# Adaptive-norm double layer: statistics closed ahead of the two joints, last tile gated by VectorE, and a drain with TensorE transposes and split tiles

## The reference

```python
h = layernorm(x) * (1 + ca) + sa;  x = x + ga * attn0(h)   # 32 heads of 16, softmax over the heads of one token
h = layernorm(x) * (1 + cb) + sb;  x = x + gb * ffn0(h)    # base + top-2 of 16 LoRA experts
h = layernorm(x) * (1 + ca1) + sa1; x = x + ga1 * attn1(h) # latent attention: 32 heads, 2 batches
h = layernorm(x) * (1 + cb1) + sb1; x = x + gb1 * ffn1(h)
# ffn1: eff_W = W + lora_B @ lora_A
#       y = h @ eff_W.T / sqrt(sum(eff_W**2, axis=1)) * magnitude
# layernorm: (x - mean) / sqrt(var + 1e-5); ga.., gb.. are pushed to at least 0.25 in magnitude
```

## Time and profile before

| what | value |
|---|---|
| time, median of 3 runs | 903.19 us (901.45 to 907.17) |
| the profiled execution | 899.29 us, span 897.1 us |
| TensorE busy | 816.5 us, 91% |
| VectorE busy | 681.6 us, 76% |
| ScalarE busy | 535.0 us, 60% |
| GpSimd busy | 538.9 us, 60% |
| block 0 ends, block 1 starts | 155.6 / 155.9 us |
| block 1 ends, block 2 starts | 283.8 / 284.1 us |
| last scores (step 255) | 838.9 us |
| mean granted TensorE clock | 0.967 of 2.4 GHz |

### The profile page before, as it was taken

One profiled execution on the slowest core, in us unless ns is written; L12 is line 12 of the kernel. 1 busy time (PEld: TensorE's weight loads), 2 busy tenths in 40 slices (PEclk: granted clock), 3 DMA queues, 4 the chain that ended last, 5 costly groups with the idle time before them and its releaser, 6 DMA issues.

```text
span 897.1 us, 15066 instructions
## 1 busy us (share of the span) xinstructions
PE 816.5 (91%) x4560; PEld 537.7 (60%) x4560; DVE 681.6 (76%) x1322; ACT 535.0 (60%) x1158; POOL 538.9 (60%) x481
## 2 busy tenths in 40 slices
PE   3899994899995997899999999999999999999997
PEld 1588873667774874565656565655656556565543
DVE  4768896835443477989989898889998889898652
ACT  5668874733323775666666666665666666665522
POOL 3333432021222237998989888887888888897213
PEclk8899997899997998999999999999999999999999
DMA  8630000494424442666666666665566766565511
GB/s 330 216 122 2 1 2 3 133 245 152 128 68 152 124 130 50 162 159 155 155 150 156 152 155 152 157 155 139 141 155 183 187 150 156 145 159 138 133 33 70
DMA packets 91459, 120.07 MB, mean 134 GB/s; under 512 B 30386, under 2 KB 41650, under 8 KB 91380
## 3 DMA queue, kind: packets, MB, share of 16 engines
q1 hardware_dynamic: 66804, 85.54, 34.5%
q10 hardware_dynamic: 24576, 33.59, 15.2%
HBM read 41.45 MB, written 2.10 MB: 49 GB/s over the span
## 4 chain that ended last, share of the span: by engine, by line
PE 42%; DVE 9%; issue 6%; ACTq 2%; ACT 2%; POOL 1%; DMA 0%; POOLq 0%; DVEq 0%; SPq 0%
PE bank L1558 10%; PE bank L1545 6%; PE bank L1546 4%; PE bank L1547 4%; PE bank L1572 4%; PE bank L1574 3%; PE bank L1573 3%; PE bank L1616 3%; DVE blk L1664 3%; ACTq L1507 2%; DVE cT_lo L1736 2%; DVE stage_a L1200 1%; DVE nmax L1648 1%; DVE stage_a L1203 1%; PE bank L1183 1%
## 5 line engine op out<-in xcount | busy, mean ns | idle before, releaser
L1648 DVE TENSOR_REDUCE nmax<-bank 128x1 f32<-128x512 f32 x256 | 174.0, 680 | 45.0 <-PE bank L1547 43.9
L1798 ACT ACTIVATE prob<-bank,nmax 128x512 f32<-128x512 f32 x172 | 118.1, 687 | 100.1 <-DVE nmax L1648 88.2
L1886 POOL TENSOR_TENSOR prob<-prob,rinv 128x512 f32<-128x512 f32 x129 | 132.6, 1042 | 31.7 <-DVE rinv L1656 29.5
L1545 PE MATMUL bank<-xk_hi,q_hi 128*128 128x512 f32 x256 | 112.9, 441 | 15.7 <-ACT prob L1798 8.8
L1664 DVE STREAM_TRANSPOSE blk<-prob 128x512 f32<-128x512 f32 x172 | 120.0, 698 | 6.5 <-ACT prob L1840 5.1
L1545 PEld LDWEIGHTS bank<-xk_hi,q_hi 128*128 128x128 f32 x256 | 48.5, 189 | 93.8 <-issue 53.8
L1546 PE MATMUL bank<-xk_lo,q_hi 128*128 128x512 f32 x256 | 101.6, 397 | 0.0
L1547 PE MATMUL bank<-xk_hi,q_lo 128*128 128x512 f32 x256 | 100.7, 393 | 0.0
L1217 POOL TENSOR_TENSOR q_lo<-stage_a,q_hi 128x512 fp32r<-128x512 f32 x64 | 82.2, 1285 | 25.4 <-ACT q_hi L1208 25.2
L1798 ACT ACTIVATE stage_a<-bank,nmax 128x512 f32<-128x512 f32 x84 | 57.7, 687 | 48.7 <-DVE nmax L1648 43.4
L1213 POOL TENSOR_TENSOR stage_a<-stage_a 128x512 f32<-128x512 f32 x64 | 82.8, 1294 | 4.8 <-DMA stage_a<-stage_a 4.8
(11 more groups left out here) (251 smaller groups left out, 1934.2 us busy)
## 6 DMA issues: line engine op xcount, KB each, us to landing
pT<-blk SPq DMA_DIRECT2D x256, 64.0 KB, 2.1
pT<-blk ACTq DMA_DIRECT2D x256, 64.0 KB, 2.1
raw_e<-blk SPq DMA_DIRECT2D x256, 64.0 KB, 2.1
raw_e<-blk ACTq DMA_DIRECT2D x256, 64.0 KB, 2.1
raw_e<-in_wo SPq DMA_DIRECT2D x16, 512.0 KB, 3.9
stage_a<-stage_a SPq DMA_DIRECT2D x128, 64.0 KB, 2.1
raw_e<-in_wmod SPq DMA_DIRECT2D x6, 1024.0 KB, 7.7
stage_a<-in_wmod SPq DMA_DIRECT2D x12, 512.0 KB, 4.7
```

The costliest lines, as they stand in the source:

```text
L1545: pe.matmul(sbk, q_hi[:, u % 2, q], xk_hi[:, 2, ks], start=True, stop=False)
L1648: dve.tensor_reduce(nmax[:, s % RING:s % RING + 1], s_bank[s % 2][:, :], AX.X, ALU.max, negate=True).then_inc(max_done, 1)
L1798: act.activation(prob[s % RING], s_bank[s % 2][:, :], ACT.Exp, bias=nmax[:, s % RING:s % RING + 1], accum_out=rsum[:, s % RING:s % RING + ...
L1886: pool.tensor_tensor(prob[s % RING], prob[s % RING], bc(rinv[:, s % RING:s % RING + 1], [P, S]), ALU.mult).then_inc(norm_pool, 1)
```

## The change

- **Joints.** `dve_next_rstd` and `act_next_std` close the statistics of tiles 0 to 6 (aggregation, root, reciprocal) at the end of the block in front, on VectorE before it finishes tile 7 and on ScalarE as its last instruction. Tile 7's gate and add move from GpSimd to VectorE; in block 1, GpSimd multiplies the bias with the gate and adds that to x earlier, and VectorE multiplies the PSUM result with the gate. The next block starts with the two normalizations; tile 7's statistics, aggregation, root and reciprocal follow inside it. ScalarE rounds the weights before it takes tile 7's root.
- **Drain.** The loop ends at step 255; what follows is written out in order. Unit 63 is turned by TensorE (`last_T`, four transposes for each 128-row tile, into free banks) and copied by VectorE (`last_turn`) instead of 16 transfers. VectorE adds the four slices of squares (`add_squares`), so that one fp32 matmul is left. Contexts of couples 30 and 31 come first on TensorE, then turns, projections and tiles. Tiles 4 to 7 use split matmuls; ScalarE rounds weights and tiles, GpSimd and VectorE make the rests. The last tile is added by VectorE. ScalarE's squares (`w_square`) move one step earlier in the loop, and its first two transfers of unit 62 ahead of the last exponential.

The diff, cut to its core:

```diff
+        def dve_next_rstd(dve, n):
+            for t in range(LAST):
+                dve.wait_ge(stat_done, TILES * n + t + 1)
+                dve.bn_aggr(mv[:, t, :], stats[:, t, :]).then_inc(norm_var, 1)
+            dve.wait_ge(norm_std, 2 * n + 1)
+            dve.reciprocal(rstd[:, 0:LAST], rstd[:, 0:LAST]).then_inc(norm_rstd, 1)
+        def act_next_std(act, n):
+            act.wait_ge(norm_var, TILES * n + LAST)
+            act.activation(rstd[:, 0:LAST], mv[:, 0:LAST, 1], ACT.Sqrt, bias=eps[:, 0:1]).then_inc(norm_std, 1)
...
 # block 0, VectorE
+                        if t == TILES:
+                            dve.wait_ge(x1_done, LAST)
+                            tile_stats(dve, LAST - 1)
+                            dve_next_rstd(dve, 1)
                         if t >= 1:
                             finish(t - 1)
...
-                    dve.wait_ge(x1_done, TILES)
-                    tile_stats(dve, TILES - 1)
+                    dve.wait_ge(otok_done, TILES)
+                    dve.tensor_tensor(o_g[:, :], o_tok[:, :], gate[:, 0, B - 1, :], ALU.mult).then_inc(last_gated, 1)
+                    dve.wait_ge(last_gated, 1)
+                    dve.tensor_tensor(x[:, LAST, :], x[:, LAST, :], o_g[:, :], ALU.add).then_inc(last_gated, 1)
...
 # block 1, ScalarE (block 2 the same with small_in and wc_hi)
-                    nrm.act_std(act)
                     act.wait_ge(ffn_in, 48)
                     for raw, hi, lo in parts[:KC]:
                         act.activation(hi, raw, ACT.Copy).then_inc(split2_hi, 1)
+                    nrm.act_last_std(act)
                     nrm.act_h(act, 0, pT)
...
+                    act_next_std(act, 2)
 # block 1, VectorE (block 2 the same without widen)
-                    widen(dve, 1, wide1)
-                    nrm.dve_stats(dve)
                     nrm.dve_xn(dve, 0)
                     nrm.dve_xn(dve, 1)
+                    nrm.dve_last_stats(dve)
+                    widen(dve, 1, wide1)
                     for n in range(KC):
                         weight_rest(n)
+                    nrm.dve_last_rstd(dve)
                     nrm.dve_lo(dve, 0)
...
+                    dve_next_rstd(dve, 2)
+                    dve.wait_ge(f_ps, 2 * TILES)
+                    dve.wait_ge(fg_done, LAST)
+                    dve.tensor_tensor(f_sum[:, :], y_bank[(TILES + 1) % 2][:, :], gate[:, 1, B - 1, :],
+                                      ALU.mult).then_inc(last_gated, 1)
+                    dve.wait_ge(last_bias, 2)
+                    dve.wait_ge(last_gated, 3)
+                    dve.tensor_tensor(x[:, LAST, :], x[:, LAST, :], f_sum[:, :], ALU.add).then_inc(last_gated, 1)
...
 # block 3, TensorE
+                    def last_T(st):
+                        s = LAST * TPB + st
+                        norm_ready(pe, s)
...
+                        for kt in range(TPB):
+                            mm = pe.transpose(tr_bank[st][:, kt * P:(kt + 1) * P], prob[s % RING][:, kt * P:(kt + 1) * P],
+                                              ident[:, :])
+                        mm.then_inc(tr_ps, 1)
...
+                            mm = split_matmuls(pe, y_bank[t % 2][:, :], [
+                                ((fh_hi[:, t % 2, c, :], fh_lo[:, t % 2, c, :]), (fw_hi[:, c, :], fw_lo[:, c, :]))
+                                for c in range(KC)])
...
+                    last_T(0)
+                    last_T(1)
+                    context(COUPLES - 2, (0, 1))
+                    context(COUPLES - 2, (2, 3))
+                    last_T(2)
+                    last_T(3)
+                    sum_squares()
+                    context(COUPLES - 1, (0, 1))
+                    context(COUPLES - 1, (2, 3))
+                    tile_T(0)
+                    project_out(COUPLES - 2, (0, 1))
+                    project_out(COUPLES - 2, (2, 3))
+                    tile_T(1)
+                    tile_y(0)
+                    project_out(COUPLES - 1, (0, 1))
+                    project_out(COUPLES - 1, (2, 3))
+                    for t in range(1, TILES):
                         if t + 1 < TILES:
                             tile_T(t + 1)
                         tile_y(t)
 # block 3, VectorE
+                        dve.tensor_copy(pT[LAST % P_SLOTS].rearrange("p g (k t q) -> p t k g q", k=TPB, t=TPB)[:, st],
+                                        tr_bank[st].rearrange("p (k g q) -> p k g q", k=TPB, g=QD)).then_inc(tr_done, 1)
...
+                    last_turn(0)
+                    row_inv(ROUNDS - 2)
+                    last_turn(1)
+                    add_squares()
+                    last_turn(2)
+                    last_turn(3)
+                    context_rest(COUPLES - 2)
+                    tile_rstd(0, TPB)
+                    tile_xn(0)
+                    tile_xn(1)
+                    norm_inverse()
+                    context_rest(COUPLES - 1)
+                    factors()
+                    tile_xn(2)
+                    tile_gate(0)
+                    tile_xn(3)
                     gated(1, 0)
...
                     tile_gate(2)
+                    tile_xn(5)
                     tile_rstd(6, 8)
+                    tile_lo(4)
                     tile_gate(3)
                     for t in range(4, TILES):
+                        if t + 1 < TILES:
+                            tile_lo(t + 1)
                         if t + 2 < TILES:
                             tile_xn(t + 2)
                         tile_gate(t)
+                    dve.wait_ge(yg_done, TILES)
+                    dve.tensor_tensor(x[:, TILES - 1, :], x[:, TILES - 1, :], y_g[:, (TILES - 1) % 2, :],
+                                      ALU.add).then_inc(x4_last, 1)
 # block 3, ScalarE
+                        if t >= TPB:
+                            act.wait_ge(f_hf, t + 1)
+                            act.activation(fh_hi[:, t % 2, :, :], f_h[:, t % 2, :, :], ACT.Copy).then_inc(f_hi, 1)
...
+                        if s == ROUNDS - 1:
+                            moves(LAST - 1, 0)
+                        exps(s)
...
+                    norm_row(ROUNDS - 1)
+                    for jj in range(1, TPB):
+                        moves(LAST - 1, jj)
+                    context_round(COUPLES - 2)
+                    tile_std(0, TPB)
+                    out_weights(COUPLES - 2)
+                    act.wait_ge(blo_done, WB_FREE)
+                    column_norm()
+                    act.wait_ge(s_ps, ROUNDS)
+                    w_round(0)
+                    w_round(1)
+                    tile_h(0)
+                    context_round(COUPLES - 1)
+                    out_weights(COUPLES - 1)
+                    tile_h(1)
+                    w_round(2)
+                    w_round(3)
+                    tile_h(2)
+                    tile_std(4, 6)
                     tile_h(3)
                     tile_std(6, 8)
+                    for t in range(TPB, TILES):
                         tile_h(t)
 # block 3, GpSimd
+                    normalize(ROUNDS - 2)
+                    out_weights(COUPLES - 2)
+                    w_rest(0)
+                    w_rest(1)
+                    out_weights(COUPLES - 1)
+                    w_rest(2)
+                    w_rest(3)
+                    for t in range(TILES - 1):
                         pool.wait_ge(yg_done, t + 1)
                         pool.tensor_tensor(x[:, t, :], x[:, t, :], y_g[:, t % 2, :], ALU.add).then_inc(x4_done, 1)
```

More of the change, by code:

```diff
@@ L473, in _ @@
                     act.wait_ge(norm_var, 2)
-                    act.activation(rstd[:, 0:2], mv[:, 0:2, 1], ACT.Sqrt, bias=eps[:, 0:1]).then_inc(first_std, 1)
+                    act.activation(rstd[:, 0:2], mv[:, 0:2, 1], ACT.Sqrt, bias=eps[:, 0:1]).then_inc(norm_std, 1)
                     row_copy(0)
@@ L912, in second_modulation @@
                         link(pool.tensor_scalar_add(mod_b3[:, CB:CB + KC, :], mod_b3[:, CB:CB + KC, :], 1.0))
-                    for t in range(TILES):
+                    for t in range(LAST):
                         pool.wait_ge(fsum_done, t + 1)
@@ L922, in _ @@
                             second_modulation()
+                    pool.wait_ge(x2_done, LAST)
+                    pool.tensor_tensor(f_g[:, :], biasf[:, :], gate[:, 1, B - 1, :], ALU.mult).then_inc(last_bias, 1)
+                    pool.wait_ge(nrm.xn, nrm.o + TILES)
+                    pool.wait_ge(last_bias, 1)
+                    pool.tensor_tensor(x[:, LAST, :], x[:, LAST, :], f_g[:, :], ALU.add).then_inc(last_bias, 1)
                 @block.scalar
@@ L1514, in _ @@
                         swap(sp, u)
-                    for u in range(UNITS):
+                    for u in range(LAST):
                         move_ready(sp, u)
@@ L1723, in _ @@
                         rotate(dve, 1, part)
-                    for s in range(STEPS):
-                        if s < ROUNDS:
-                            row_max(s)
```

(28 more changed lines are left out.)

223 lines of the change are left out of this document (117 added, 106 removed).

## The result

The changed kernel takes 895.15 us, median of 4 runs (890.95 to 897.59), against 903.37 of the kernel before (4 runs, 901.45 to 907.17): a ratio of 0.9896 with an interval of 0.9852 to 0.994. The forecast was 894.5. The profiled execution took 897.59 us (span 895.4), only 1.7 us less in span than the one before it, so the first thing to do with the two traces is to cut them at the same events.

What follows compares the result with a forecast made beforehand. TensorE bounds the head loop and most of the drain, the VectorE, GpSimd, ScalarE chain the joints. 3.2 + 0.35 + 5.15 = 8.7 us off the 903.19 median gives 894.5; own range 892 to 898, overall 889 to 900.5.

Steps and rivals of the forecast that it cites:

- Joint 1: Block 0 to block 1: VectorE's gate and add, with earlier statistics, bring the first modulation 3.2 us earlier; bounds 2.0 and 3.6.
- Rival (e): At joint 1 the rearranged statistics give nothing; only the drain's 5 us remain, 898.2; chance 6%.
- Joint 2: Block 1 to block 2: start 2.8 us earlier, but the last small load leaves 0.35; bounds −1.0 and +0.8.
- Rival (c): Small loads land in time at joint 2, or joint 1 unblocks later loads: gain 11 to 12.5 us, 891.4; chance 6%.
- The head loop: Squares of the last weights one step earlier on ScalarE delay exponentials once by 0.63 us; nothing is lost.
- The drain: Last unit to end of span: TensorE bounds it, then the last three tiles' loop; gain 5.15 us, bounds 3.3 and 6.3.
- Rival (a): Drain's front late: the second context waits for unit 62's last landing or ScalarE's queue; gain 6.2 us, 897.0; chance 15%.
- (d): Clock falls to 1.2 GHz before the drain's second context and stays or returns late: 3.0 us slower, 906.2; chance 8%.
- the rule of the Trainium skill: Transposes do not count as TensorE activity as matmuls do, so the new drain could fall to the lower clock.
- The loop of 4.15 a tile: Drain's last three tiles: turn, modulation, rounding, low part, next normalization take 4.15 us a tile against TensorE's 3.2.
- rival (b): Drain's split tiles run at TensorE's pace, 3.2 us a tile: gain 11.5, 891.7; chance 10%.
- all ready before TensorE asks: Drain before the last tiles' loop: VectorE's and ScalarE's work, including normalization 5 at 870.8, never holds up TensorE.

Runs made afterwards that it cites:

- the run with the joints alone: New blocks 0 to 2 of the changed kernel with block 3 of the kernel before: 899.97 us, ratio 0.9975.
- the sixth: Changed kernel with VectorE's normalization of tile t+2 put before the low part of tile t+1 in its last loop: 894.28 us, ratio 0.9890.
- with the loads first: Changed kernel with block 2's five small loads issued ahead of the last couple's load on SP's queue: 892.02 us, ratio 0.9883.
- The run with the drain alone: Blocks 0 to 2 of the kernel before with the changed kernel's block 3: 898.91 us, ratio 0.9952.
- the second pair: Both kernels profiled once more, unchanged: 901.3 us for the kernel before, 899.28 us for the changed one.
- the run with the rests moved: Changed kernel with GpSimd's four rests of the weights moved behind its first addition to x: 894.2 us, ratio 0.9899.
- the runs without the rests beside it: Changed kernel with GpSimd's weight rests moved later, 894.2 us; and with tiles 4 to 7 as plain fp32, no rests, 897.45 us.
- the run with everything together: Changed kernel with small loads first, VectorE's next normalization first, and tile 4's modulation ahead of ScalarE's second root: 891.49 us, ratio 0.9861.

## Why the prediction was right

**Joint 1, 3.2 forecast, 3.3 measured.** Both parts of the argument hold: two VectorE instructions in place of GpSimd's, and the seven tiles' statistics under the context that VectorE waits for anyway. Rival (e) falls: the run with the joints alone has the 3.3 too.

**Joint 2, 0.35 forecast, 0.3 to 0.7 measured in five profiles of six, and 0.9 lost in the sixth.** The step that looked like 2.8 was cut down to the landing of the last small load. That was right: with the loads first the joint is 3.7 shorter. The size hangs on how soon that load lands, 4.8 in the forecast, 4.6 to 5.0 in the five and 6.2 in the sixth, which is inside the forecast's bound of −1.0. What reaches the head loop is smaller still (59.55 against 59.74). Rival (c), that the loads land in time anyway, falls by the 6.67 us that ScalarE waits for them.

**The head loop, 0 forecast.** 499.97 against 500.34, and 502.21 against 500.30 in the second pair. The run with the drain alone has 503.41, but the run with the joints alone, whose head loop is the old one, has 502.36, and two runs with the new loop have 497.09 and 497.34. A cost of up to some 2 us can't be excluded by these, nor a gain; what differs between executions of one kernel is as large. The clock near the loop's end, where TensorE pauses for the last rows, differs too. In the second profile of the changed kernel it read:

```profile
836.00:844.00 8.00, 7.24 (x15) 0.57 0.38 91
```

In the same place it is 0.79 in the first profiles of both kernels, and 1.00 in the second of the kernel before, which with 500.30 is no faster than the first. So the clock there doesn't account for the spread by itself, and the rest is open.

**The drain, 5.15 forecast, 4.1 measured.** Its front came out to the hundredth: second context 8.39 after the last row maximum, forecast 8.39; copy 0.65, forecast 0.65. Rival (a), a late landing, happened once, in the run with the rests moved (0.78 late), but isn't the changed kernel's normal state. The clock stayed at 1.00, so (d) falls, and the rule of the Trainium skill weighed beside it (TensorE: Matmul & The Clock Gate, Part 4, on transposes) had no effect here: TensorE is busy 19 of 20 us in the new drain, turns among the work in all of it. The loop of 4.15 a tile was the step that mattered most against rival (b), and it came: 4.25 and 4.10. The 4.10 has the normalization as releaser and shrinks to 3.22 when the normalization is put first. The 4.25 was forecast by this loop alone, and there luck helped: the 0.66 wait for y(4), which the forecast did not have, makes 4.12 by itself.

What failed in the drain is the sentence that VectorE's and ScalarE's work is "all ready before TensorE asks". The turn of tile 5 was forecast 33.58 after the last row maximum and came at 34.13; the turn of tile 2 waited 0.35 for its normalization, where the sign was to be no wait before y(4). I had taken every VectorE duration from rows in which GpSimd was idle or in which one operand was in PSUM. The drain puts GpSimd's rests of weights beside VectorE's work from SBUF: 0.97 more for the two factors and 0.85 more for one normalization, of which 0.57 reach TensorE, as the runs without the rests beside it show. The other part is at the end: from the first pass of tile 7 (888.42) to its gate on VectorE (891.51) it took 3.1 where I had 12 passes of 0.23, 2.8. The second pass starts 0.34 behind the first (888.76), and the last one takes 0.39 from its start at 891.09 to its end. Together 0.9 of the missing 1.0. The 0.66 wait for y(4) cost little on top, as the loop by way of VectorE took 0.13 longer than the path through that wait. Rival (d) has a slip in its working, four turns at 1.1 in one place and at 0.85 in another; nothing hangs on it.

**The sum.** Forecast 8.7; by the steps 3.3 + 0.5 + 4.1 = 7.9; by the medians 8.2, by the ratio 9.4 with 4.0 on either side. That 895.15 came within 0.7 of the forecast's 894.5 is therefore partly luck; the steps are the test of the argument. The chance of 0.54 for a change within 1% and 0.42 for more was fair: the ratio of 0.9896 lies just beyond 1% and its interval on both sides of it.

## What to carry to other kernels

When work leaves a bottleneck, look for the transfer that was landing "just then": here 2.3 of 2.8 us were waiting behind a load whose issue had not moved, and moving its issue was worth more than the edit of the engines. Then look whether the gain is still there at the next wait. A cheaper operation on TensorE that needs a rounding and a rest from two other engines is worth only what their loop leaves; in such a loop put the work that releases the next turn ahead of the work that finishes this one. Judge edits of a few microseconds by the step between two events of the trace; the whole span carries several microseconds that belong to no edit.

## What was not expected of the hardware

**VectorE and GpSimd on SBUF.** With GpSimd working, VectorE's normalization (one tile from SBUF) took 1.40 instead of 0.54, and in the run with everything together a difference of two SBUF tiles 1.75 instead of 0.69. The rows of that run, first GpSimd, then VectorE:

```profile
867.55 1.50 POOL L2072 TENSOR_TENSOR x_res<-x_res,wb_all 128x512 f32<-128x512 f32 x1 [2.14 <-DVE wb_all L1836]
```

```profile
867.85 1.75 DVE L1790 TENSOR_TENSOR q_lo<-wb_all,q_hi 128x512 fp32r<-128x512 f32 x1
```

The slow VectorE row starts within GpSimd's and ends 0.55 after it: 869.60 against 869.05. In the changed kernel the normalization of 1.40 (863.29) ends 0.28 after GpSimd's two rests (864.69 against 864.41). It looks as if VectorE first waited GpSimd out and then did its own work, and the profile books the wait as duration. VectorE's products with one operand in PSUM are not slowed; in the changed kernel two of them beside GpSimd's addition take 1.28, 0.64 each:

```profile
865.37 1.50 POOL L2069 TENSOR_TENSOR x_res<-x_res,wb_all 128x512 f32<-128x512 f32 x1 [0.96 <-DVE wb_all L1834]
865.67 1.28 DVE L1756 TENSOR_TENSOR bank<-bank,gate 128x512 f32<-128x512 f32 x2
```

It goes the other way round too. GpSimd's addition takes 1.50 where it starts under a VectorE normalization, as here (865.22 to 865.75), and 1.29 where it does not. The Trainium skill, SBUF — State Buffer, Who interferes with whom, has this as a lock: the port pair that the two engines share goes to one of them for a whole instruction, for VectorE operations with two SBUF inputs or in a two-port mode. The trace agrees, the product with one input in PSUM included; in which mode the normalization, with its one SBUF tile, was run, no trace shows.

**The start of the kernel.** In the profile of the changed kernel the same 512-column matmuls that take 0.39 at 30 us in the profile of before take 0.63, and the distance between two of them is 0.43 instead of 0.23. That is the lower clock level by their pace (a 512-column pass took 0.43 at 836.07 in the earlier trace rows, in a window of 836 to 838 at 0.50), though the clock column reads 1.00 there. The windows, before and then after:

```profile
30.00:40.00 10.00, 8.70 (x103) 6.04 (x101) 7.84 (x15) 9.85 (x15) 4.07 (x3) 1.00 0.28 81
```

```profile
30.00:40.00 10.00, 10.00 (x38) 7.76 (x38) 4.07 (x2) 7.28 (x10) 6.15 (x3) 1.00 0.01 2
```

From 10 to 20 us the same 36 matmuls keep TensorE busy 5.35 us in the one and 7.50 in the other. The slower pace goes with the 6.2 us by which that execution ends its block 0 late. Over all eleven profiles the start follows the clock of 20 to 30 us: the five that start at 147.6 to 148.2 read 0.67 to 0.72 there, the four at 149.9 to 152.6 read 0.50, one of them the kernel before, and the two at 154.1 and 154.2 have the slow pace under a column of 1.00. In this stretch the pace of the matmuls has to be read, not the column; why the column differs was not settled.
